# Encoder half turn in another order: input transposes a quarter in, query and key projections in the middle, maxima denser early

## The chip, the cores and the metric

The kernel runs on one core of a Trainium2 chip. The metric is the device time of one execution in microseconds (us), as the median of three runs.

## The reference, cut to what matters

The model embeds image patches and text, runs a four-layer text encoder over the text (8 batches of 512 tokens, width 192, 12 heads of 16), then one attention block over image and text together, then a mixture of eight experts. The change lies in the encoder alone:

```python
def layer(h, p):
    q = heads(h @ wq + bq_); k = heads(h @ wk + bk_); v = heads(h @ wv + bv_)
    scores = jnp.einsum('bhqd,bhkd->bhqk', q, k) / jnp.sqrt(jnp.float32(dk))
    attn = jax.nn.softmax(scores, axis=-1)
    o = jnp.einsum('bhqk,bhkd->bhqd', attn, v)
    o = o.transpose(0, 2, 1, 3).reshape(B, S, D)
    h = _ln(h + o @ wo + bo_, g1_, bn1_)
    ff = jax.nn.relu(h @ w1 + b1_) @ w2 + b2_
    h = _ln(h + ff, g2_, bn2_)
```

## The kernel before, in words

The phases stand one behind the other: embedding, encoder, attention, experts. In the encoder (`encoder_phase`, L344) a batch and layer is one unit of work, and two units are in flight, in slots 0 and 1. The program is a list of steps, made of half turns: `half_steps(s)` (L277) interleaves six streams of steps, and the string `ORDER` (L269) says, letter by letter, from which stream the next step is taken. All five engines walk this one list in its order, each doing what a step asks of it, and wait for one another by counting semaphores. In half turn s, with o = 1 - s the other slot:

- e: 24 steps `exp n.x` of slot s, named e n.x below. PE computes 128 keys by 512 queries of scores for two heads (L491, two matmuls on separate rows of the array), ACT takes the exponential into `probs` (L605). n counts six pairs of tiles; `probs` has two buffers, for n even and n odd.
- p: pv0 to pv5, values times probabilities (L505, 16 matmuls); pv n waits for ACT's last exponential of e n. After each second one ACT moves the sum out of PSUM (ev, L576).
- m: 24 steps `max t.i` of slot o, named m t.i below: PE computes scores again, two heads of 128 queries (L478), and DVE reduces each row to its maximum (L691). The 25th is maxt: PE transposes the maxima (L483), ACT negates them (L592), and ACT itself issues the two DMAs (L597) that put them into a row of `q_stack`, where the exponentials of the next half turn find them.
- j: the next unit of slot s: tx (8 transposes of the input, L458; ACT copies them to `hT`, L583; POOL splits that in three instructions, L752 to L756), qk0 to qk2 (query and key projections, L441, ACT L590, DVE L665), v0 and v1 (values, L470, DVE L684). qk0 waits for POOL's split. Behind qk2 SP spills the projections to DRAM and loads them as stacks for the next half turn's maxima and the exponentials after those.
- h: the rest of slot o's attention: nt0, nt1 (transposes, L514; DVE L678, L679), ot (L520, ACT L581), wo0, wo1 (L530; DVE adds and takes moments, L698 to L648; POOL takes the reciprocal root, L49 and L51), ln1 (DVE L656, then three instructions of POOL, L776 to L783).
- f: slot o's feed-forward: ft (transposes, L536, waits for POOL's ln1; ACT L608, DVE L670, L671), six f1 (L441; ACT L611, L612), four f2 (L551), ln2.

Every step with a PSUM product holds one of three buffers (`RING`, L157) from its first matmul until ACT or DVE has read it; the buffers go round in the order in which they were closed. v, wo, f1 (by pairs) and f2 hold theirs over several steps. 32 half turns make the encoder: two whole ones written out after a first without h and f, 26 in a hardware loop, and two at the end with parts left out (`AHEAD`, `FIRST`, `BODY`, `FINAL`, `CLOSE`, L313 to L317). 29 of them are whole.

Of the kernel before, what the change touches and what calls it, by code (L numbers as in the profile page):

```python
# [265 lines left out]

ORDER = "jeehemehememhmepemhemheepheejeppmemememmfepmmfefmjmpjemmfmffefmepemfemfmmpmfmfjjfp"  # L269
JOBS = ("tx", "qk", "v", "max", "maxt", "exp", "nt", "ot", "wo", "ft", "f1", "f2")  # L270
ON_ACT = ("tx", "qk", "maxt", "exp", "ev", "ot", "ft", "f1")
ON_DVE = ("qk", "v", "max", "nt", "wo", "ft", "f2")
# [4 lines left out]
def half_steps(s, without=""):  # L277
# [7 lines left out]
        "f": [("ft", o)] + [("f1", o, m, j) for m in range(3) for j in range(2)] + [("f2", o, i) for i in range(4)] + [("ln", o, 2)]}  # L285
    assert sorted(ORDER) == sorted(k for k, v in streams.items() for _ in v)
    left, out = {k: iter(v) for k, v in streams.items()}, []
    for k in ORDER:
        step = next(left[k])
# [1720 lines left out]
```

## Time and profile before

| | us |
|---|---|
| median of 3 runs | 4592.13 (4589.54 to 4593.84) |
| the profiled execution | 4594.65 |
| its span, first to last instruction | 4592.5 |
| encoder, from the first input transpose (98.45) | to about 2260 |

| engine | busy, share of the span |
|---|---|
| PE (matmul) | 3869.3 us, 84% |
| DVE | 2150.8 us, 47% |
| ACT | 2117.4 us, 46% |
| POOL | 1147.7 us, 25% |

The mean granted clock of TensorE is 0.92 of full speed. Times are counted from the span's start. A view "by stretches" gives each engine's busy time between two times, with the granted clock (1.00 is 2.4 GHz, 0.5 would be 1.2 GHz throughout). In a timeline a row gives the start, the time taken, the engine, the line, the operation and, in brackets, the idle time of the engine before it and who ended it; matmul ends are modelled, so starts are what is compared.

### The profile page before, as it was taken

Reading aid. Unit: us, or ns where it says so; the run is one execution under the profiler, and the core shown is the slowest. Engines: PE = TensorE matmul, PEld = TensorE weight load, DVE = VectorE, ACT = ScalarE, POOL = GpSimd, SP = SyncE. Lnnn points to the kernel's source line nnn. Section 1 sums busy time; section 2 is a strip of 40 time slices with the busy share of each in tenths; the row PEclk is TensorE's granted clock in tenths of the full one; section 3 lists DMA queues with packets and bytes.
Section 4 is the critical chain, followed back from the end, with each engine's and each line's share of the span. In section 5 each row is a group of like instructions: output and inputs, shape, how many; then the busy total and the mean of one; then the engine's idle time right before and its main releaser. Section 6 shows DMA issues by size and latency. Waiting matters only on the chain. (4 is left out here: it accounts for less than half of the span.)

```text
span 4592.5 us, 66354 instructions
## 1 busy us (share of the span) xinstructions
PE 3869.3 (84%) x21988; PEld 2541.8 (55%) x21988; DVE 2150.8 (47%) x3265; ACT 2117.4 (46%) x3304; POOL 1147.7 (25%) x1126
## 2 busy tenths in 40 slices
PE   1799999999999999999849999999999963099990
PEld 1355555555555555555436767767667743088880
DVE  2566666656666656666435444444445423011112
ACT  0355455545545544544516676566666630022220
POOL 4123323323332322332210010010000010633326
PEclk6799999999999999999969999999999985599995
DMA  6323333332433232233011111111111132455544
GB/s 134 115 79 94 114 97 91 104 101 84 97 111 95 85 114 88 78 114 101 22 43 29 25 29 38 27 29 36 27 26 38 29 102 76 94 165 153 159 130 124
DMA packets 306312, 378.52 MB, mean 82 GB/s; under 512 B 63559, under 2 KB 209415, under 8 KB 305927
## 3 DMA queue, kind: packets, MB, share of 16 engines
q1 hardware_dynamic: 258967, 284.95, 22.5%
q0 software_dynamic: 23168, 73.32, 6.1%
q10 hardware_dynamic: 24016, 18.09, 1.2%
q8 instruction: 103, 1.69, 0.2%
q14 instruction: 58, 0.48, 0.0%
HBM read 245.69 MB, written 101.30 MB: 76 GB/s over the span
## 5 line engine op out<-in xcount | busy, mean ns | idle before, releaser
L691 DVE TENSOR_REDUCE mx<-ring 128x2 f32<-128x1024 f32 x768 | 919.7, 1223 | 486.4 <-PE ring L478 483.1
L605 ACT ACTIVATE probs<-ring 128x1024 f32<-128x1024 f32 x768 | 767.7, 1024 | 411.9 <-PE ring L491 410.6
L1421 DVE TENSOR_REDUCE a_nmx<-a_ring 128x1 f32<-128x561 f32 (+1 forms) x480 | 341.7, 737 | 308.1 <-PE a_ring L1270 159.2
L1319 ACT ACTIVATE a_ring<-a_ring,a_nmx 128x561 f32<-128x561 f32 (+1 forms) x480 | 333.8, 695 | 196.9 <-DVE a_nmx L1421 193.9
L478 PE MATMUL ring<-k_stack,q_stack 48*128 48x512 f32 x1536 | 359.6, 479 | 55.4 <-DVE mx L691 23.2
L491 PE MATMUL ring<-q_stack,k_stack 64*128 64x512 f32 x1536 | 358.4, 484 | 54.4 <-DVE mx L691 39.5
L505 PE MATMUL acc<-probs,vals 128*32 128x512 f32 x3072 | 393.9, 633 | 1.3 <-ACT probs L605 1.3
L1200 POOL TENSOR_SCALAR_AFFINE_SELECT a_probs<-a_probs 128x256 f32<-128x256 f32 (+1 forms) x240 | 91.9, 383 | 1208.4 <-ACT a_probs L1351 1208.4
L1351 ACT ACTIVATE a_probs<-a_ring 128x561 f32<-128x561 f32 (+1 forms) x480 | 287.3, 637 | 169.4 <-PE a_ring L1267 166.5
L1267 PE MATMUL a_ring<-a_k_hh,a_q_hl 128*128 128x256 f32 (+1 forms) x960 | 310.4, 338 | 23.0 <-DVE a_q_hl L1401 11.0
L1267 PE MATMUL a_ring<-a_q_hl,a_k_hh 128*128 128x256 f32 (+1 forms) x960 | 287.4, 325 | 10.4 <-ACT a_ring L1319 7.6
L491 PEld LDWEIGHTS ring<-q_stack,k_stack 64*128 64x128 f32 x1536 | 140.4, 189 | 280.8 <-DVE mx L691 97.4
L478 PEld LDWEIGHTS ring<-k_stack,q_stack 48*128 48x128 f32 x1536 | 146.0, 191 | 270.3 <-DVE mx L691 84.0
L551 PE MATMUL ring<-w,relu 128*128 128x192 f32 x1536 | 279.8, 333 | 1.4 <-ACT relu L612 1.4
L1287 PE MATMUL a_acc<-a_probs,a_vals 128*64 128x305 f32 (+1 forms) x1920 | 273.3, 411 | 0.1
L1267 PE MATMUL a_ring<-a_k_l,a_q_hm 128*128 128x256 f32 (+1 forms) x960 | 271.5, 292 | 0.0
L551 PEld LDWEIGHTS ring<-w,relu 128*128 128x128 f32 x1536 | 246.4, 190 | 33.6 <-issue 31.1
L1267 PE MATMUL a_ring<-a_q_hm,a_k_l 128*128 128x256 f32 (+1 forms) x960 | 263.8, 292 | 0.0
L1812 PE MATMUL m_ring<-m_xT,m_wup 96*128 96x256 f32 x1056 | 247.0, 384 | 16.6 <-DVE m_xT L1859 7.8
L1841 ACT ACTIVATE m_hid<-m_ring,m_bup 128x256 f32<-128x256 f32 x264 | 122.7, 473 | 263.1 <-PE m_ring L1812 263.0
L49 POOL TENSOR_SCALAR var_eps<-mv 128x4 f32<-128x4 f32 x64 | 14.6, 228 | 873.5 <-DVE mv L648 873.5
L1812 PEld LDWEIGHTS m_ring<-m_xT,m_wup 96*128 96x128 f32 x1056 | 197.5, 192 | 46.9 <-DVE m_xT L1859 10.3
(206 smaller groups left out, 6575.2 us busy)
## 6 DMA issues: line engine op xcount, KB each, us to landing
q_stack<-qk_scratch SPq DMA_DIRECT2D x576, 64.0 KB, 2.4
k_stack<-qk_scratch SPq DMA_DIRECT2D x576, 64.0 KB, 2.5
qk_scratch<-qk_hi SPq DMA_DIRECT2D x32, 768.0 KB, 3.7
qk_scratch<-qk_lo SPq DMA_DIRECT2D x32, 768.0 KB, 5.2
a_q_hm<-a_q_hl SPq DMA_DIRECT2D x48, 280.5 KB
a_k_hh<-a_k_hh SPq DMA_DIRECT2D x48, 280.5 KB
h_in<-tokens SPq DMA_DIRECT2D x34, 384.0 KB, 4.4
res<-tokens SPq DMA_DIRECT2D x32, 384.0 KB, 3.4
```

The lines of the kernel that those rows point to most:

```text
L478: last = nc.tensor.matmul(buf[:, r, :], q_st[s][terms, t, P * i:P * i + P], k_st[s][terms, t, :], start=True, stop=True)
L491: last = nc.tensor.matmul(buf[:, r, :], k_st[s][terms, t, P * kt:P * kt + P], q_st[s][terms, t, :], start=True, stop=True)
L505: last = nc.tensor.matmul(acc[g % 2][32 * hh:32 * hh + 32, :], vals[s][:, kt, 4 * (n // 2) + hh, :], probs[n % 2][:, hh, j, :], start=(n % ...
L551: last = nc.tensor.matmul(buf[:, i // 2, D * (i % 2):D * (i % 2) + D], relu[:, k2, P * i:P * i + P], w2[:, k2, :], start=(k2 == 0), stop=( ...
L605: nc.scalar.activation(probs[n % 2][:, pair:pair + 2, x // 2, :], buf[:, :, :], ACT.Exp, scale=DK ** -0.5).then_inc(act, 1)
L691: nc.vector.tensor_reduce(mx[s][:, i, :].rearrange("p (r t) -> p r t", r=2)[:, :, t], buf[:, :, :], AX, ALU.max).then_inc(dve, 1)
L1267: last = nc.tensor.matmul(flat(buf)[0:r, n0:n0 + w], a, b[:, n0:n0 + w], start=(m == 0), stop=(m == 1 and not masked))
L1287: last = nc.tensor.matmul(flat(acc)[DH * r:DH * r + DH, n0:n0 + w], vals[:, i, 2 * p + r, :], probs[i][:, r, n0:n0 + w], start=(i == 0), s ...
L1319: nc.scalar.activation(buf, buf, ACT.Exp, bias=nmx[0:r, i, h:h + 1], accum_out=sums[0:r, i, h:h + 1]).then_inc(act, 1)
L1351: nc.scalar.activation(probs[i][0:r, h % 2, :], flat(buf)[0:r, 0:N], ACT.Exp).then_inc(act, 1)
L1421: nc.vector.tensor_reduce(nmx[0:r, i, h:h + 1], flat(buf)[0:r, 0:N], AX, ALU.max, negate=True).then_inc(dve, 1)
L1812: last = nc.tensor.matmul(buf[:, 0, 0:BLOCK], wup[b][:, c, P * m:P * m + P], xT[b][:, c, :], start=(c == 0), stop=(c == 1))
```

## The change

Only `ORDER` changes; the same 82 steps stand in another order.

```diff
-ORDER = "jeehemehememhmepmemhemheepheejeppmemememmfepmmfefmjmpjemmfmffefmepemfemfmmpmfmfjjfp"
+ORDER = "ehehememmhmmpeehmmheeejmheemmpempmejeepemfjepmmjfmfmfemffmmfmeefmpefmefmfmfeppjjp"
```

Spelled out for PE (f1 numbered by its two digits, "|" is only a mark for the eye):

```
before  tx e0.0 e0.1 nt0 e0.2 m0.0 e0.3 nt1 e1.0 m0.1 e1.1 m0.2 ot m0.3 e1.2 pv0 e1.3 m1.0 wo0 e2.0 m1.1 wo1
        | e2.1 e2.2 pv1 e2.3 e3.0 qk0 e3.1 pv2 m1.2 e3.2 m1.3 e3.3 m2.0 e4.0 m2.1 m2.2 ft e4.1 pv3 m2.3 m3.0
        | f1_00 e4.2 f1_01 m3.1 qk1 m3.2 qk2 e4.3 m3.3 m4.0 f1_10 m4.1 f1_11 f1_20 e5.0 f1_21 m4.2 e5.1 pv4 e5.2
        | m4.3 f2_0 e5.3 m5.0 f2_1 m5.1 m5.2 pv5 m5.3 f2_2 maxt f2_3 v0 v1
after   e0.0 nt0 e0.1 nt1 e0.2 m0.0 e0.3 m0.1 m0.2 ot m0.3 m1.0 pv0 e1.0 e1.1 wo0 m1.1 m1.2 wo1
        | e1.2 e1.3 e2.0 tx m1.3 e2.1 e2.2 m2.0 m2.1 pv1 e2.3 m2.2 m2.3 e3.0 qk0 e3.1 e3.2 pv2 e3.3 m3.0 ft qk1
        | e4.0 pv3 m3.1 m3.2 qk2 f1_00 m3.3 f1_01 m4.0 f1_10 e4.1 m4.1 f1_11 f1_20 m4.2 m4.3 f1_21 m5.0 e4.2 e4.3
        | f2_0 m5.1 e5.0 f2_1 m5.2 e5.1 f2_2 m5.3 e5.2 f2_3 maxt e5.3 pv4 pv5 v0 v1
```

The steps without PE move too: ln1 stands between m1.3 and e2.1 (before: behind pv1), ln2 right behind maxt (before: behind v1), the three ev behind m2.2, m5.1 and v1 (before: e3.1, m3.2 and ln2).

## Rows read from the trace of the kernel before

**Rows 1.** By stretches: start:end, length, busy PE, PEld, DVE, ACT, POOL, clock, DMA
```profile
224.41:290.33 65.92, 62.29 (x358) 35.06 (x357) 40.98 (x56) 34.31 (x40) 13.92 (x12) 1.00 0.28 82
...
1231.73:1297.86 66.13, 62.30 (x359) 35.17 (x358) 42.10 (x60) 34.35 (x40) 21.90 (x16) 1.00 0.31 92
1297.86:1365.25 67.39, 63.70 (x359) 35.84 (x358) 42.08 (x60) 34.34 (x40) 19.64 (x16) 0.97 0.36 104
...
224.41:2113.12 1888.71, 1785.06 (x9998) 999.57 (x9997) 1177.68 (x1676) 961.46 (x1120) 575.56 (x417) 0.97 0.34 97
2113.12:2180.17 67.05, 63.26 (x357) 35.43 (x356) 42.08 (x60) 34.33 (x40) 19.13 (x16) 0.97 0.36 103
```

**Rows 2.** Waits of PE, 224.41 to 2180.17: total us, times, longest
```profile
PE ring L491 <- DVE mx L691: 36.0, 58, 0.9
PE ring L478 <- ACT probs L605: 21.3, 57, 0.5
```

**Rows 3.** Timeline of PE, 1253 to 1260, in the half turn that starts at 1231.73
```profile
1254.60 0.50 PE L478 MATMUL ring<-k_stack,q_stack 48*128 48x512 f32 x2
...
1256.43 0.51 PE L491 MATMUL ring<-q_stack,k_stack 64*128 64x512 f32 x2 [0.85 <-DVE mx L691]
...
1259.34 1.09 PE L536 MATMUL ring<-ident,h 128*128 128x128 f32 x8
```

**Rows 4.** Timeline of PE, 1320 to 1330, the same place of the half turn from 1297.86
```profile
1325.42 1.97 PE L536 MATMUL ring<-ident,h 128*128 128x128 f32 x8
```

**Rows 5.** Timeline of DVE and ACT, consumers of the score steps
```profile
1255.15 5.81 DVE L691 TENSOR_REDUCE mx<-ring 128x2 f32<-128x1024 f32 x5 [0.93 <-PE ring L478]
...
1233.79 3.88 ACT L605 ACTIVATE probs<-ring 128x1024 f32<-128x1024 f32 x4
1244.01 1.02 ACT L605 ACTIVATE probs<-ring 128x1024 f32<-128x1024 f32 x1 [1.16 <-PE ring L491]
```

**Rows 6.** Timeline of PE, 1240 to 1252, costs of steps start to start
```profile
1241.19 0.50 PE L491 MATMUL ring<-q_stack,k_stack 64*128 64x512 f32 x2
1241.62 1.92 PE L505 MATMUL acc<-probs,vals 128*32 128x512 f32 x16
1243.47 0.50 PE L491 MATMUL ring<-q_stack,k_stack 64*128 64x512 f32 x2
...
1244.13 1.57 PE L530 MATMUL ring<-wo,oT 96*128 96x192 f32 x8
```

**Rows 7.** Timeline of all engines, 1291 to 1298, end of a half turn
```profile
1291.41 0.60 PE L483 MATMUL ring<-ident,mx 128*12 128x128 f32 x4
...
1292.04 0.58 ACT L592 ACTIVATE oT<-ring 12x512 fp32r<-12x512 f32 x1 [6.89 <-PE ring L483]
1292.73 1.42 ACTq L597 DMA_DIRECT2D q_stack<-oT  x2
...
1294.27 0.60 ACT L576 ACTIVATE o_raw<-acc 128x512 f32<-128x512 f32 x1 [1.65 <-PE ring L551]
```

**Rows 8.** Timeline of DVE and POOL, 1248 to 1260, and POOL's split of the input
```profile
1248.07 0.96 DVE L698 TENSOR_TENSOR y<-ring,res 128x768 f32<-128x768 f32 x1 [0.44 <-PE ring L530]
...
1251.24 1.04 POOL L51 TENSOR_TENSOR rstd<-var_eps,half 128x4 f32<-128x4 f32 x1
...
1257.45 1.83 POOL L783 TENSOR_TENSOR res<-h,enc_rows 128x768 f32<-128x768 f32 x1
...
1239.47 1.04 POOL L752 CAST hT_hi<-hT 128x1024 fp32r<-128x1024 f32 x1
...
1241.95 1.28 POOL L756 TENSOR_TENSOR hT_hi<-hT,hT_hi 64x512 fp32r<-64x512 f32 x1
```

**Rows 9.** Timeline of PE, 1293 to 1298 and 2176 to 2181: v before tx, v before e0.0
```profile
1293.80 4.13 PE L470 MATMUL ring<-wv,hT 128*128 128x192 f32 x16
...
2176.62 3.97 PE L470 MATMUL ring<-wv,hT 128*128 128x192 f32 x15
...
2180.46 0.75 PE L491 MATMUL ring<-q_stack,k_stack 64*128 64x512 f32 x3
```

More of the change, by code:

```diff
@@ L258, in freed @@
         return name, self.reached(it, name, i)
-ORDER = "jeehemehememhmepemhemheepheejeppmemememmfepmmfefmjmpjemmfmffefmepemfemfmmpmfmfjjfp"
+ORDER = "ehehememmhmmpeehmmheeejmheemmpempmejeepemfjepmmjfmfmfemffmmfmeefmpefmefmefmfeppjjp"
 JOBS = ("tx", "qk", "v", "max", "maxt", "exp", "nt", "ot", "wo", "ft", "f1", "f2")
```

## The prediction

> **What bounds the kernel now.** I read the view by stretches first, cut at the start of each tx, so that each stretch is one half turn; then PE's waits, then the timelines around the places that the change moves. In the encoder PE is busy for 62.30 of 66.13 us of a half turn, DVE for 42.10, ACT for 34.35 [rows 1]. PE sets the time, and a half turn is PE's own work, its short waits, and what a lower clock adds. The waits are for a free buffer: PE has three, and stands until DVE has reduced a maximum (36.0 us in 58 waits before L491, two in each half turn) or ACT has taken an exponential (21.3 us in 57) [rows 2]. The worst place is the run m1.2 to m2.2: eight score steps with nothing else between them, from 1254.60 to ft at 1259.34 [rows 3]. By the rates below PE needs 0.43 + 7 x 0.23 = 2.04 us for eight such steps; the other 2.7 us of those 4.74 it stands, because the five maxima among them take DVE 5.81 us [rows 5].
>
> The clock is the second thing to see. The 29 whole half turns take 1888.71 + 67.05 = 1955.8 us [rows 1]. Ten of them show a clock of 1.00 and take 66.1, as those at 224.41 and 1231.73 do; the others show less and take more, as 67.39 at 0.97 [rows 1]. So 1955.8 - 29 x 66.13 = 38 us, 0.8% of the kernel, is what the clock takes. Where it falls is plain in a timeline: the transposes of ft, directly behind the run of eight, took 1.09 us at 2.4 GHz [rows 3] and 1.97 in the half turn from 1297.86 [rows 4], which is the rate of 1.2 GHz. Before that, PE had done eight sparse score steps.
>
> **The change, part by part.** No instruction is added or removed; steps move, with their DMAs. I replay the new order by hand, by these rates. A score step alone among full-array steps costs PE 0.43 us (1241.19 to 1241.62), two together 0.66 (1243.47 to 1244.13), so each further one 0.23 [rows 6]; pv costs 1.85 [rows 6]. ACT starts 0.54 after the matmul (1243.47 to 1244.01) [rows 5, 6] and frees after 1.02, and in a row needs (3.88 - 1.02) / 3 = 0.95 for each; DVE needs 1.23, in a row (5.81 - 1.23) / 4 = 1.145 [rows 5]. A freed buffer lets PE start 0.05 later: the first maximum ends at 1256.38, e3.3 starts at 1256.43 [rows 3, 5]. Times now count from e0.0 in the new order.
>
> *Start, to pv0.* nt0 no longer waits for ACT's copy of tx. e0.1 waits for v's buffer until 1.35, m0.0 is at 3.04, then DVE and ACT hand out buffers: e0.3 3.64, m0.1 4.20, m0.2 4.82, ot 5.33, m1.0 7.16 (the longest wait, 0.49), pv0 7.59. Seven waits, 1.6 us.
>
> *wo1 to pv1.* wo1 ends at 13.81. e1.3 waits for m1.2's reduction until 14.57 (0.42), e2.0 for DVE's sum of wo until 15.52 (0.62), tx 15.95, m1.3 16.97, e2.1 17.30, e2.2 for ACT's copy of tx until 18.19 (0.55), m2.0 18.87 (0.35), m2.1 19.20, pv1 19.53 to 21.39. Two waits of 0.36 follow among e2.3 to e3.0, and qk0 starts at 23.54.
>
> *POOL.* tx's split now stands between wo1's root and ln1. DVE starts wo1's sum at 14.50; the root is ready 4.21 later (1248.07 to 1252.28) [rows 8], at 18.7; the split takes 3.76 (1239.47 to 1243.23) [rows 8], to 22.5, ahead of qk0; ln1 5.65 more, to 28.1. ft would come at 28.06 by itself and waits 0.1 at most. If POOL were 1 us later, ft would be, too: no cover is left there.
>
> *Middle, qk0 to f2.* Maxima stand in ones and twos; ft and qk1, qk2 and f1_00 are neighbours. I find 0.1 at qk0 and then no wait until e4.2, which stands behind m4.2, m4.3, m5.0: 0.61, e4.3 0.17, f2_0 0.29. f2_3 ends at 57.15.
>
> *End.* Here a wait is added. maxt stands ahead of e5.3, pv4, pv5. On ACT the negation starts 0.63 behind maxt's matmuls (1291.41 to 1292.04), then ACT issues two DMAs of its own, 1292.73 to 1294.15, and its next work starts at 1294.27 [rows 7]: 2.86 behind maxt. e5.3's exponential is queued behind that, and pv5 waits for it: 2.86 + 1.02 + 0.06 = 3.94 behind maxt. PE has maxt 0.53, e5.3 0.43, pv4 1.75 (no change of array shape behind it, so 0.1 less): 2.71. PE stands 1.23 us, each half turn. Before, the same DMA time hid beside f2_3 and v, since pv5 was done.
>
> *Half turn's seam.* v before tx costs 4.06 (1293.80 to 1297.86); v before e0.0, which the last half turns show, 3.84 (2176.62 to 2180.46) [rows 1, 9]: 0.22 saved. Hidden at no cost: maxt's DMAs (9 us until e0.0 wants them, 7 before); ln2 now ends before the half turn's seam; the third stacks are issued behind e5.3, 6 us later, but m4.0 is half a turn away; on SP these DMAs pass only h_out's store, which nobody waits for.
>
> The sum is 66.67 us for a half turn at full clock, against 66.13: 20 waits of 6.8 us in all, and 59.9 of work. 29 x 0.54 = 15.7 us **lost**. Twenty waits, each read to 0.05 or less, leave +-0.35 on a half turn, +-10 us in all.
>
> *The clock.* The run of eight is gone. Its nearest successor is e1.2 to m2.1, eight score steps and tx between wo1 and pv1, in 19.53 - 13.81 = 5.72 us; but tx is 1.03 us of transposes inside it, so by the rates above PE works for 0.89 + 1.03 + 1.35 = 3.3 of 5.7 us there, where it worked for 2.0 of 4.7. The start has five score steps between nt1 and ot. The starts of before, thick with waits as well but with transposes between, kept the clock in 27 or so of 29 half turns; what fell was the run without them. I take two falls at 38 / 19 = 2 us in place of nineteen: 34 us **won**, bounds 0 (all nineteen stay) and 38 (none).
>
> The Trainium skill speaks against this: "TensorE: Matmul & The Clock Gate", section "A second HAM failure mode: psum-queue depth-cycling", says that a PE which idles for moments between groups of matmuls while it cycles through PSUM buffers swings between its two clocks. By that, 20 waits are no better than the ones before, and the nineteen falls stay; the trace agrees that such a cycle does it, but shows it at one place.
>
> Ends of the encoder: the first half turn, and those without j or m, have other gaps; the first loses tx as filler under maxt's DMA. Between -2 and +5, I take +2 (nearest: one pv5 wait more in each). Sum: 15.7 - 34 + 2 = -16, on the profiled 4594.65: 4578; on the median of 4592.13, 2.5 lower: 4576. I say 4577.
>
> **Rivals.** (1) *The clock falls as often as before*, now between wo1 and pv1. The waits there speak for it; tx inside, and the starts that held, against. Then 15.7 + 2 = +18: about 4611. It decides from some 14 falls on: there the loss passes the bound of 9 us. (2) *The replay is too short*: another 0.3 to 0.5 us for each half turn, most likely where POOL has no cover, at ft. +9 to +15 on the forecast: 4586 to 4592, no change. (3) *pv5 does not wait*, because ACT's queue lets the exponential pass its own DMA issue. The row of L576, ready long before and held until 1294.27 [rows 7], speaks against. 1.23 x 29 = 36 less: 4541.
>
> **How the numbers follow.** Forecast, 4560 to 4586: 0.53. Rival 1: 0.18, rival 2: 0.23, rival 3: 0.06. A measurement tells 0.2%, 9.2 us, from no change. Faster by more (under 4583): 0.48 of the forecast's and rival 3's and a little of rival 2, 0.56 in all; slower (over 4601): 0.19; within: 0.25. The range goes from 4558, the replay 0.3 shorter with no fall, to 4609, most of rival 1.
>
> **What would show it.** Right: half turns of 66.7 at a clock of 1.00; PE waiting before L505 for ACT's L605 some 1.2 us in each of 29 to 31 half turns, a wait that before doesn't have; ft without falls behind it. Wrong: a clock of 0.97 or less in more than ten half turns; ft waiting for POOL by more than 0.3; full-clock half turns over 67.1 or under 66.3.

## The result

The changed kernel takes 4702.12 us (median, 4699.66 to 4706.83) against 4592.99 of the kernel before beside it: a ratio of 1.0235 [1.0220, 1.0251]. It is slower by 109 us, where 16 us less were forecast, and it lies outside the range. The profiled execution took 4699.66 us, with a span of 4697.6, 105.1 more than before.

The view by stretches, one half turn from e0.0 to e0.0 (columns as in [rows 1]):

```profile
1225.99:1297.63 71.64, 65.12 (x360) 35.74 (x359) 44.74 (x60) 34.65 (x40) 19.59 (x16) 0.98 0.33 87
```

It is 71.64 us at a clock below 1.00, and the 29 behind the first, taken from maxt to maxt, lie between 70.99 and 72.06. Before it was 66.13 at a clock of 1.00, or 67.39 with a fall [rows 1]; forecast was 66.67 at 1.00. One number more has moved: DVE is busy for 44.74 us, not 42.10, with as many instructions as before. Some instruction of DVE takes longer. PE's waits say where that hurts (224 to 2300; total us, times, longest):

```profile
PE ring L478 <- DVE mx L691: 87.7, 113, 2.2
PE acc L505 <- ACT probs L605: 30.2, 29, 1.1
PE ring L491 <- DVE mx L691: 13.8, 40, 0.4
```

The wait of rows 2 for DVE before L491 has gone from 36.0 to 13.8, as the order meant; in its place PE waits 87.7 us before L478, up to 2.2 at once. No row names ft waiting for POOL. The second row is pv5's wait behind ACT's DMA issue, 29 times, 1.04 on average, where 1.23 was forecast. The timeline at the end of a half turn, ACT and PE, has it (ACT's part answers to [rows 7]):

```profile
1217.88 1.41 ACTq L597 DMA_DIRECT2D q_stack<-oT  x2
1219.40 1.02 ACT L605 ACTIVATE probs<-ring 128x1024 f32<-128x1024 f32 x1 [1.63 <-issue]
1220.48 1.92 PE L505 MATMUL acc<-probs,vals 128*32 128x512 f32 x16 [1.05 <-ACT probs L605]
```

The timeline of PE shows the place of the 2.2:

```profile
1245.89 1.92 PE L505 MATMUL acc<-probs,vals 128*32 128x512 f32 x16
1247.75 0.49 PE L491 MATMUL ring<-q_stack,k_stack 64*128 64x512 f32 x2
1250.27 0.49 PE L478 MATMUL ring<-k_stack,q_stack 48*128 48x512 f32 x2 [2.02 <-DVE mx L691]
1251.40 0.50 PE L478 MATMUL ring<-k_stack,q_stack 48*128 48x512 f32 x2 [0.64 <-DVE mx L691]
...
1252.74 0.47 PE L441 MATMUL ring<-hT_hi,wqk_hi 128*128 128x512 f32 x1 [0.61 <-DVE mx L691]
...
1255.74 2.43 PE L505 MATMUL acc<-probs,vals 128*32 128x512 f32 x16
```

These are pv1, e2.3, m2.2, m2.3, qk0 and pv2. Count from e0.0 at 1225.99: pv1 starts at 19.90, where the replay has 19.53; qk0 starts at 26.75, where it has 23.54. Between them PE stands for DVE three times, and behind that the clock falls: pv2 takes 2.36 us until the next step (1258.10) and not 1.85.

The timeline of DVE and POOL in the same microseconds shows why:

```profile
1245.01 4.07 DVE L656 TENSOR_SCALAR yn<-y,mv,rstd 128x192 f32<-128x192 f32 x4
1249.00 4.60 DVE L691 TENSOR_REDUCE mx<-ring 128x2 f32<-128x1024 f32 x4
...
1244.93 1.04 POOL L752 CAST hT_hi<-hT 128x1024 fp32r<-128x1024 f32 x1
1246.05 1.28 POOL L754 TENSOR_TENSOR hT_lo<-hT,hT_hi 128x512 fp32r<-128x512 f32 x1
1247.41 1.27 POOL L756 TENSOR_TENSOR hT_hi<-hT,hT_hi 64x512 fp32r<-64x512 f32 x1
1249.16 1.81 POOL L776 TENSOR_TENSOR h<-yn,enc_rows 128x768 f32<-128x768 f32 x1 [0.48 <-DVE yn L656]
```

DVE's four `yn` of ln1 took 4.07 us. Taken one by one from the trace, they and POOL's three instructions of the split stand so:

```
DVE  yn 1  1245.008 to 1246.086      POOL L752  1244.934 to 1245.971
DVE  yn 2  1246.007 to 1247.444      POOL L754  1246.053 to 1247.329
DVE  yn 3  1247.365 to 1248.790      POOL L756  1247.407 to 1248.673
DVE  yn 4  1248.712 to 1249.080      (POOL idle until 1249.16)
```

Each of the first three ends 0.115 to 0.117 us behind the end of a POOL instruction, and so do the three of every other whole half turn, 87 in all, within 0.112 to 0.122. The fourth, with POOL idle, takes 0.37. POOL's three take 1.04, 1.28 and 1.27, as they did before [rows 8]: it is DVE alone that loses. Then the reductions, queued behind them on DVE, start at 1249.00. They run beside POOL's L776 and take 1.15 each, which is their usual rate in a row [rows 5]. So POOL holds up `yn`, which reads and writes SBUF, and not the reduction, which reads PSUM.

### The profile page after: what moved, and what is told of

The parts are those of the page before. It is cut to its first block and busy times, and to the rows that moved or that the text cites. A ratio compares the mean times of both kernels' runs of the same rounds, so it can differ in the third digit from the quotient of the medians.

```text
span 4697.6 us, 66419 instructions
## 1 busy us (share of the span) xinstructions
PE 3908.3 (83%) x21988; PEld 2540.7 (54%) x21988; DVE 2227.7 (47%) x3265; ACT 2126.3 (45%) x3304; POOL 1146.5 (24%) x1126
## 5 line engine op out<-in xcount | busy, mean ns | idle before, releaser
L691 DVE TENSOR_REDUCE mx<-ring 128x2 f32<-128x1024 f32 x768 | 907.3, 1220 | 496.2 <-PE ring L478 495.8
L478 PE MATMUL ring<-k_stack,q_stack 48*128 48x512 f32 x1536 | 370.9, 497 | 103.5 <-DVE mx L691 99.2
L491 PE MATMUL ring<-q_stack,k_stack 64*128 64x512 f32 x1536 | 381.3, 497 | 56.8 <-DVE mx L691 17.1
L478 PEld LDWEIGHTS ring<-k_stack,q_stack 48*128 48x128 f32 x1536 | 145.7, 189 | 308.4 <-DVE mx L691 180.6
L491 PEld LDWEIGHTS ring<-q_stack,k_stack 64*128 64x128 f32 x1536 | 152.1, 196 | 282.9 <-issue 136.1
```

What stands on the lines that cost most here:

```text
L478: last = nc.tensor.matmul(buf[:, r, :], q_st[s][terms, t, P * i:P * i + P], k_st[s][terms, t, :], start=True, stop=True)
L491: last = nc.tensor.matmul(buf[:, r, :], k_st[s][terms, t, P * kt:P * kt + P], q_st[s][terms, t, :], start=True, stop=True)
L691: nc.vector.tensor_reduce(mx[s][:, i, :].rearrange("p (r t) -> p r t", r=2)[:, :, t], buf[:, :, :], AX, ALU.max).then_inc(dve, 1)
```

## The experiments

Theory A: POOL's split, side by side with DVE's `yn`, holds it up; that delays the maxima, PE stands, and the clock falls because it stood. Rival B: the split and ln1 come too late in POOL's and DVE's queues, whatever runs beside them. Rival C: the order of the score steps alone makes the waits and the falls.

### The split made small

```diff
-nc.gpsimd.tensor_copy(hT_hi[:, :, :], hT[:, :, :])...
+nc.gpsimd.tensor_copy(hT_hi[:, :, 0:8], hT[:, :, 0:8])...
```

and so in the two subtractions. The kernel leaves out the split of all columns behind the eighth, which are set to zero once at the start.

> The changed kernel with POOL's three instructions that split the input (L752 to L756) cut from 512 columns to 8; the rest of the split input stays zero, so the projections are wrong and nothing else. Theory 1 (lock): in the changed kernel DVE's four instructions of ln1 (L656, 4.07 us in place of 1.25) stand because POOL's split runs beside them and holds something that both need; with the split gone they take 1.25 again, m2.0 comes some 2.5 us earlier, PE's 2.0 us gap before it goes, and with it the fall of the clock: half turns of 66.7 to 67.3, in all 4565 to 4590. Theory 2 (queue): ln1 costs because it stands between m1.3 and m2.0 in DVE's order, behind a root that POOL gives late; how long the split takes doesn't matter: half turns stay over 70.5, in all over 4670.

4577.64 us, 0.9960 [0.9946, 0.9974] of before. The order is that of the change, and its loss is gone. One half turn by stretches, from e0.0 to e0.0:

```profile
1229.43:1296.83 67.40, 63.57 (x358) 35.24 (x357) 42.01 (x60) 34.60 (x40) 18.89 (x16) 1.00 0.35 104
```

DVE's `yn` in the timeline of the same half turn:

```profile
1248.36 1.25 DVE L656 TENSOR_SCALAR yn<-y,mv,rstd 128x192 f32<-128x192 f32 x4
```

PE's waits, from 224 to 2300:

```profile
PE acc L505 <- ACT probs L605: 31.5, 31, 1.1
PE ring L478 <- DVE mx L691: 14.9, 55, 0.4
```

`yn` takes 1.25 again, PE's wait before L478 falls from 87.7 us to 14.9, and the clock holds at 1.00 in every half turn from the third to the last but one. Rival C falls. The same edit in the kernel before:

> The kernel before with the same three instructions cut to 8 columns, the same part of the computation left out: the control. There the split runs beside reductions that read PSUM, and qk0 comes 8 us behind it. Both theories: no change within 0.3%, 4580 to 4605. Should it be faster by more than 15 us, cutting the split is worth something by itself, and that is to be taken off what the other run shows.

4587.41 us, 0.9993 [0.9980, 1.0005]: there the split costs nothing that shows in the half turns, and its falls of the clock stay. It does bring the first maxt forward (ACT's L592 starts at 156.29 us and not at 161.26, and at 155.67 in the run above), since ahead of the loop PE waits for the split; so about 5 us of both runs are due to the smaller split alone, and the order without the collision stands at some 4583, an estimate from these two runs.

### POOL's three instructions made six

```diff
-nc.gpsimd.tensor_copy(hT_hi[:, :, :], hT[:, :, :])...
+for c0 in (0, 256):
+    nc.gpsimd.tensor_copy(hT_hi[:, :, c0:c0 + 256], hT[:, :, c0:c0 + 256])...
```

and so in the two subtractions: as many bytes, in twice as many instructions.

> The changed kernel with each of POOL's three split instructions made into two of 256 columns: six instructions, the same bytes and about the same time in all (some 0.3 us more). Theory 1 in its form of a lock held for one whole instruction: each of DVE's four waits for one POOL instruction of half the length, so L656 takes some 2.4 to 2.9 us in place of 4.07, and a half turn loses 1.2 to 2 us: 4640 to 4670. In the form of shared bandwidth (DVE slowed for as long as POOL runs): no change of L656, 4695 to 4715.

4628.96 us, 1.0077 [1.0058, 1.0097], below what either theory gave. The timeline of DVE and of POOL:

```profile
1208.24 2.76 DVE L656 TENSOR_SCALAR yn<-y,mv,rstd 128x192 f32<-128x192 f32 x4
...
1208.17 1.20 POOL L753 CAST hT_hi<-hT 128x512 fp32r<-128x512 f32 x2
1209.45 1.44 POOL L756 TENSOR_TENSOR hT_lo<-hT,hT_hi 128x256 fp32r<-128x256 f32 x2
```

All `yn` of the run, by their line (duration ns min/median/max; the maximum of the changed kernel is 1451):

```profile
L656 DVE TENSOR_SCALAR yn<-y,mv,rstd x256: 370/379/900, 243.4 to 2391.4; 128x192 f32<-128x192 f32 x128
```

The four take 2.76 us and not 4.07, and the longest 0.90 and not 1.45. Sharing of bandwidth would leave both as they were, for POOL moves the same bytes in no less time. One instruction of POOL is waited out, and then DVE has its turn: all four now end 0.11 to 0.12 us behind one, in each of the 29 half turns. PE's waits:

```profile
PE ring L478 <- DVE mx L691: 50.4, 113, 0.6
```

Half turns are 68.7 us, and 21 of 29 keep the clock at 1.00. With the longest wait there 0.6 us and not 2.2, the clock mostly holds; that the falls of the changed kernel come from how long PE stands is argued from this and from the run with the small split, in which it holds in every whole half turn.

### The two kept apart, nothing left out

```diff
 await_step(g, R, it, "act", step, now + 1)
+for k in range(now + 1, min(now + 5, len(R.steps))):
+    if R.steps[k][0] == "ln" and R.steps[k][2] == 1:
+        g.wait_ge(ln, R.done(it, "ln", R.steps[k], k + 1))
```

> The changed kernel with one wait more: POOL's split of tx waits until DVE has written the four yn of ln1, so the two can't run side by side. No work is left out. Collision theory (the lost 5 us of a half turn are DVE's yn held by POOL's split, and the clock fall that follows): L656 takes 0.37 us each again, no clock fall between wo1 and pv2, and what it costs is POOL's chain, 1.3 us later: qk0 0.25 and ft 1.2 to 1.4 us later in each half turn by my replay, 29 x 0 to 1.6 us on the 4577 us of the run with the small split: 4577 to 4625. If the loss came from the split being late rather than from the collision, this run is later still and takes over 4700.

4620.11 us, 1.0057 [1.0040, 1.0073], in the range of A; B's 4700 is off. No `yn` takes more than 0.38 us. The split starts later than in the changed kernel, and the run is 82 us faster. Half turns are 68.8 at a clock of 1.00. What is left of the loss has rows of its own in PE's waits:

```profile
PE ring L536 <- POOL res L786: 37.6, 29, 1.4
...
PE ring L441 <- POOL hT_hi L759: 7.2, 26, 0.3
```

ft waits 1.3 us for POOL's ln1, and qk0 0.28 for the split: 44.8 us, against 40.9 between the spans of this run and that with the small split. That is POOL's chain, 1.3 later, without cover at ft, as the prediction had it.

> As c1_split_behind_yn, and qk1 stands ahead of ft, so that PE has 0.9 us of other work while POOL finishes ln1. If ft waits for POOL in c1_split_behind_yn, this is 0.5 to 1.0 us faster in each half turn: 15 to 30 us less than that run. If ft doesn't wait there, no difference.

```diff
-ORDER = "...pemfjepmm..."
+ORDER = "...pemjfepmm..."
```

4588.44 us, 0.9987 [0.9974, 1.0001]: 32 us less than the run before it, a little over what was expected. qk1 covers POOL's ln1; half turns are 67.65.

> As c2_qk1_first, and e5.3 ahead of maxt, so that its exponential isn't queued behind ACT's two DMAs and pv5 doesn't wait (1.05 us in 29 half turns). If the clock stays at 1.00 this gives 26 to 30 us less than c2_qk1_first: 4545 to 4580. If the wait ahead of pv5 only moves to the next half turn's start, as in a5_e53_first where half of it came back as clock falls, no gain.

```diff
-ORDER = "...fmfeppjjp"
+ORDER = "...femfppjjp"
```

(with both other edits). 4558.50 us, 0.9913 [0.9883, 0.9943], faster than both kernels, with the whole computation done. Another 30 us: pv5's wait falls from 31.6 us to 0.3, and half turns are 66.5. Three of the 29 whole ones take 69 or more from maxt to maxt and show a fall of the clock. In these PE stood first at e0.0, for 1.11, 1.95 and 2.20 us, for maxt's DMA (the fourth wait of this row is behind the whole half turns):

```profile
PE ring L491 <- DMA q_stack<-oT: 7.3, 4, 2.2
```

With e5.3 ahead of it and no wait at pv5, maxt stands 7.76 us before e0.0 and not 9.44 as in the run before, so this DMA has less cover.

### Other ways apart, and the clock

The same two sides can be parted by order alone. tx ahead of pv0:

```diff
-...hmmpeehmmheeejmhee...
+...hmmjpeehmmheeemhee...
```

> The changed kernel with tx moved from behind e2.0 to ahead of pv0, some 8 us earlier; nothing left out. POOL's split then ends before DVE's sum of wo starts. Theory 1 (lock): L656 takes 1.25, half turns of 66.5 to 67.3, in all 4560 to 4590. Theory 2 (queue): ln1 is where it was in DVE's order and m2.0 still waits 2 us: over 4670.

4644.83 us, 1.0107 [1.0090, 1.0123]: `yn` at 0.38 at most, yet far from A's 4560 to 4590. The collision was taken away and another cost came: with tx gone from between, eight score steps stand bare behind wo1, and the clock falls in 28 of the 29 whole half turns. PE's timeline, e1.2 to pv1:

```profile
1211.84 0.50 PE L491 MATMUL ring<-q_stack,k_stack 64*128 64x512 f32 x2
...
1216.17 0.73 PE L478 MATMUL ring<-k_stack,q_stack 48*128 48x512 f32 x4 [0.38 <-DVE mx L691]
1216.83 3.49 PE L505 MATMUL acc<-probs,vals 128*32 128x512 f32 x16
```

No wait in that row of steps is longer than 0.42; pv1 behind it takes 3.49 us, the rate of 1.2 GHz, and the half turn 69.3 or, with a longer fall, 70.35. In the run with the small split the same eight steps stand with the 1.03 us of tx among them, also with five waits, which add up to 0.97 us and not to 1.61 as here, and the clock holds.

ln1 behind pv1:

```diff
-...hmmheeejmheemmpe...
+...hmmheeejmeemmphe...
```

> The changed kernel with one letter moved: ln1 stands behind pv1, as before, in place of ahead of e2.1; tx stays. By the lock, DVE now reduces m2.0 and m2.1 while POOL splits, and comes to ln1 some 22 us into the half turn, when the split has 0.5 us left: L656 takes 1.3 to 2.0, PE's gap ahead of m2.2 goes, the clock holds. POOL's ln1 ends later, near 29.5, so ft waits 0.5 to 1.3 us for it. Half turns of 67.5 to 68.8: 4580 to 4620. If instead the place of tx (a split late in the half turn) costs by itself, it stays over 4650.

4615.85 us, 1.0042 [1.0028, 1.0057], inside A's range, at its upper end. It is qk0, and not ft as expected, that now waits: 1.1 us in 29 half turns for a reduction that is queued behind ln1 on DVE (31.7 us in PE's waits). One `yn` in a half turn still meets POOL's last split instruction (1231 ns at most).

e5.3 ahead of maxt in the changed kernel, the collision left as it is:

```diff
-...fmfeppjjp
+...femfppjjp
```

> The changed kernel with e5.3 ahead of maxt, nothing else. Theory of the prediction: pv5's wait (1.05 us in 29 half turns) is ACT's own DMA issue ahead of e5.3's exponential; it goes, and nothing takes its place, since e0.0 is 8 us away: 4702 less 30 to 37, so 4663 to 4675. Rival: pv4 and pv5 then wait for something else (ACT's ev, the ring), less than 10 us gained: over 4690.

4675.94 us, 1.0172 [1.0132, 1.0211], 26 less than the change: pv5's wait is worth what it shows in the rows (30.2 us), less what longer falls of the clock take back: the clock is 0.95 in 13 of 29 half turns, against 7 in the changed kernel.

Two tries to put all of this into one order, with no wait added. The first:

```diff
-...hmmpeehmmheeejmheemmpempmejeepemfjepmm...fmfeppjjp
+...hmmjpeehmmheeejmheemmpempmejeepemfepmm...femfppjjp
```

> The changed kernel with tx ahead of pv0, qk0 in tx's place, qk1 in qk0's, and e5.3 ahead of maxt. The split is over before ln1 (L656 1.25), the run of eight score steps that appeared with tx moved alone is broken by qk0, pv5 doesn't wait. If a run of eight bare score steps is what lowers the clock, and only that, half turns are 66.0 to 66.9 at full clock: 4525 to 4560. If the clock falls wherever waits are dense, also in the six steps from e2.3 to e3.2 or those around qk0, 4570 to 4620.

4605.80 us, 1.0023 [1.0007, 1.0039]. tx stands early, qk0 in its place as filler, qk1 in qk0's, and e5.3 ahead of maxt. Half turns that keep the clock take 66.9, but 24 of 29 take 68.2 or more: e2.2 now waits 0.98 for qk0's buffer, m2.0 0.63 for a maximum, and pv1 behind them runs at the low clock (3.04 us).

The second:

```diff
-...hmmheeejmheemmpempmejeepemfjepmm...fmfeppjjp
+...hmmheeejmeemmphempmejeepemjfepmm...femfppjjp
```

> The changed kernel with ln1 behind pv1, qk1 ahead of ft (so that ft has cover while POOL does ln1) and e5.3 ahead of maxt. Expected: 0.5 to 1 us less for each half turn at ft than with ln1 moved alone, 1.1 less at pv5: half turns of 66.0 to 67.2, 4525 to 4570. If POOL's ln1 is later than thought and ft waits 1 us or more, 4570 to 4600.

4609.43 us, 1.0028 [1.0011, 1.0045]. Half turns are 67.1 with the clock held, and 68.0 or more in 24 of 29, with the fall at qk0. Neither try came under 4570: the first lies in the second of its ranges, the one with falls, and this one above both of its own. It is instructive: between wo1 and qk0 it has the same steps and five waits of the same size (0.15 to 1.17 us) as the run with ln1 alone behind pv1, whose clock held in all but 4 of 29. PE's timeline at qk0, here:

```profile
1201.94 0.50 PE L491 MATMUL ring<-q_stack,k_stack 64*128 64x512 f32 x2 [0.65 <-ACT probs L605]
1203.62 0.77 PE L441 MATMUL ring<-hT_hi,wqk_hi 128*128 128x512 f32 x1 [1.17 <-DVE mx L691]
```

and with ln1 alone behind pv1:

```profile
1208.86 0.50 PE L491 MATMUL ring<-q_stack,k_stack 64*128 64x512 f32 x2 [0.65 <-ACT probs L605]
1210.56 0.47 PE L441 MATMUL ring<-hT_hi,wqk_hi 128*128 128x512 f32 x1 [1.20 <-DVE mx L691]
```

The first product takes 0.77 us in the one and 0.47 in the other. The two orders differ only elsewhere: here qk1 stands ahead of ft, some 60 us before this place, and e5.3 ahead of maxt, some 30 us before it, which takes pv5's wait away. One of these or both turned a stretch that keeps the clock into one that loses it; which, and how, was not taken apart.

## Why the prediction was wrong

**The step that failed is POOL's.** It said: the split takes 3.76 between the root and ln1, ft waits 0.1 at most; and it costs nothing else. The order on POOL and its durations were right, and ft did not wait. But a step was priced as if only its own queue counted. The split of [rows 8] ran beside reductions only. For `yn` the prediction names no time, but its qk0 at 23.54 comes out with 1.25 us for the four, which is what they took before, at 1252.31, with POOL idle beside them. The replay then let ln1's `yn` and the split start in the same moment, at the end of the root. There DVE pays 4.07 - 1.25 = 2.8 us. The Trainium skill states it, in "SBUF — State Buffer", section "Who interferes with whom": a `tensor_scalar` from SBUF to SBUF can take a second pair of ports that is GpSimd's only one, and whoever comes second is blocked for the whole instruction, which a reduction never is. The traces agree, with 0.37 against 1.08 to 1.45 us of one `yn`; which of the two came first they do not show. The prediction did not weigh that page.

**What the collision costs.** Against the run with the small split, from e0.0: qk0 is at 26.75 and not 24.06, 2.7 us, for DVE's delay has no cover among m2.2, m2.3 and qk0; then the fallen clock takes 0.5 at qk0, 0.5 at e3.1 and e3.2 and 0.5 at pv2, 1.5 us. The sum of 4.2 is 71.64 - 67.40; in 29 half turns that is 123 us, and the profiled spans differ by 120.5. So the collision, with the fall of the clock behind it, accounts for more than the 109 us lost.

**Rival 1** (the clock falls as often) came true in its sign, and more: in each half turn. But it was not the cause in that form. A fall cost 1.5 us, for the 2 taken; its condition, waits between wo1 and pv1, did not decide: each step from wo1 to pv1 stands within 0.1 us of the same place with the small split, at a clock of 1.00. The rule of the Trainium skill that the prediction weighed ("TensorE: Matmul & The Clock Gate", section "A second HAM failure mode: psum-queue depth-cycling"), on a PE that idles between groups of matmuls while it cycles through buffers, doesn't decide here by itself: PE stands 3.8 of 67.40 us with the small split, in many short waits, and not one of 28 half turns loses its clock. A stop of 2 us did lose it, and so did a bare row of score steps.

**The replay** was short (rival 2, in size, at another place). With the small split a half turn takes 66.87 us where the code is written out (277.78 to 411.51) and 67.4 in the loop, against 66.67 forecast: 0.73 x 29 = 21 us. 0.3 of it come before pv0 (7.87 for 7.59). The 0.5 that the loop has over the written-out half turns come in small gaps: 0.25 up to qk0, 0.26 at f1_00 and the rest around v. No run explains them. Rival 2's place, ft, was not it.

**The clock** term was right, with the collision away: no fall in place of nineteen, 38 us for the 34 taken.

**pv5's wait**: 1.04 for 1.23, and worth 26 to 30 us when it was taken away, where rival 3 priced 36. Its mechanism stands: e5.3's exponential starts at 1219.40, right behind ACT's two DMA issues, 1217.88 with 1.41 us, though its scores were there at 1217.58.

**The ends** were taken as +2 and are a gain: the first half turn, maxt to maxt, went from 59.29 to 53.66 us, and what follows the last maxt from 2349.8 to 2341.1, together 14 us (taken at ACT's L592). With the collision away these are 4.9 and 4.8. The ends and the first maxt are then nearly all that is won: the 29 whole half turns take 1953.5 us with the small split (219.67 to 2173.18), against 1955.8 before. 2 us were won there, and not the 18 forecast.

So 4583 without the collision lies close to the forecast, but partly by errors that cancel: 21 us of the replay against 12 of the ends and 4 of the clock. (The range's lower end, 4558, is also some 5 us under what its own terms give, 4576 - 8.7 - 4 = 4563.)

## What to carry to other kernels

When a step is moved on one engine, look at what it will now run beside on every other engine, and take its duration from a row in which the same two ran beside each other; where no such row exists, price it from nothing to the length of the other's instruction. Here a `tensor_scalar` from SBUF to SBUF on VectorE and an instruction of GpSimd were such a pair, while a reduction that reads PSUM was not; no other vector operation on SBUF alone ran beside GpSimd in these rows. Keep such a pair apart by a wait, or put work that reads PSUM beside GpSimd, and give the delayed chain other PE work to hide behind. After taking away a wait, look again at where the clock falls and at what the wait had covered; several of these edits gave some of it back there.

## What the runs showed of the hardware

- DVE waits out a whole instruction of POOL: a `yn` of 0.37 us lasted until 0.112 to 0.122 us behind the end of POOL's instruction of 1.04 to 1.28, in 87 of 87 cases. With POOL's instructions halved, the four cost 2.76 us and not 4.07. The wait shows as a longer instruction of DVE, and only what then waits for DVE has a row among the waits.
- In the order of the records `yn` 2 and 3 start 0.04 us before the POOL instruction that they then wait out (for `yn` 2, 1246.007 and 1246.053). Which of them had asked first can't be read from starts that overlap the end of the `yn` ahead; it stays open.
- The clock fell behind eight score steps with no wait over 0.42 us and 1.61 us of waits in all, and held with a tx among them and 0.97 us of waits.
- A stretch with the same steps and waits of the same size kept the clock in 25 of 29 half turns of one kernel and lost it in 24 of 29 of another, whose order differs only 30 and 60 us earlier. What is in the stretch does not decide alone.
